# A post-norm decoder layer on one core: PSUM banks dealt by block, smaller stages in another order, layer norms applied on ScalarE

## What is computed

```
x = layernorm(x + attn(x))          # 8-bit rounded activations, sign weights; 16 heads of 32;
                                    # softmax over the HEADS of one token, plus a recurrent state:
                                    # out = softmax(q k^T) v + q @ kv_state   (a state per 128-token chunk)
                                    # then rmsnorm, 8-bit rounding and a sign-weight projection
x = layernorm(x + xattn(x, ctx))    # 32 query heads, 8 kv heads of 16, window 64, keys from ctx and x
x = layernorm(x + ffn(x))           # x @ base_w^T + bias + 2.0 * LoRA, top 2 of 8 experts by softmax gate
```

## Time and profile before

| | us |
|---|---|
| median of 3 runs | 1296.49 (1296.21 to 1297.39) |
| the profiled execution, by its own clock | 1297.64 |
| its span, first to last instruction | 1295.5 |
| PE busy | 923.4 (71%) |
| DVE busy | 551.9 (43%) |
| ACT busy | 286.3 (22%) |
| POOL busy | 87.0 (7%) |
| mean granted clock of TensorE | 0.812 of full speed |

### The profile page before, as it was taken

One profiled execution on the slowest core, in us unless ns is written; L12 is line 12 of the kernel. 1 busy time (PEld: TensorE's weight loads), 2 busy tenths in 40 slices (PEclk: granted clock), 3 DMA queues, 4 the chain that ended last, 5 costly groups with the idle time before them and its releaser, 6 DMA issues.

```text
span 1295.5 us, 23211 instructions
## 1 busy us (share of the span) xinstructions
PE 923.4 (71%) x10038; PEld 604.3 (47%) x10038; DVE 551.9 (43%) x1105; ACT 286.3 (22%) x549; POOL 87.0 (7%) x103
## 2 busy tenths in 40 slices
PE   2555865867687777867777867778767876778575
PEld 2342753356434653356433754356533664355323
DVE  3425145442644346443644247443545336132322
ACT  4112212412042111412032211401132210411220
POOL 0101001010001001010001001010000100000001
PEclk9756886988888867988778877988779787888686
DMA  9501000000000000000000000000000000000000
GB/s 315 137 2 33 2 1 1 1 33 2 17 1 34 2 1 17 2 34 2 1 17 26 9 2 17 1 34 2 2 17 17 1 2 17 2 1 1 17 1 17
DMA packets 18818, 27.15 MB, mean 21 GB/s; under 512 B 5401, under 2 KB 7577, under 8 KB 18721
## 3 DMA queue, kind: packets, MB, share of 16 engines
q1 hardware_dynamic: 18432, 24.84, 6.1%
q10 hardware_dynamic: 288, 0.80, 0.2%
HBM read 21.44 MB, written 4.19 MB: 20 GB/s over the span
## 4 chain that ended last, share of the span: by engine, by line
PE 41%; issue 30%; DVE 18%; ACT 7%; POOL 2%; DMA 2%; DVEq 0%; POOLq 0%; SPq 0%; ACTq 0%
PE ps L859 9%; DVE max_b L1181 4%; PE ps L899 4%; PE ps L869 3%; ACT p_b L648 2%; PE ps L879 2%; PE ps L832 2%; PE ps L776 2%; PE ps L805 2%; PE ps L808 2%; PE ps L932 2%; PE ps L796 2%; PE ps L964 1%; ACT p_a L599 1%; DVE x L1157 1%
## 5 line engine op out<-in xcount | busy, mean ns | idle before, releaser
L1181 DVE TENSOR_REDUCE max_b<-ps 128x4 f32<-128x768 f32 (+2 forms) x160 | 105.7, 711 | 128.8 <-PE ps L913 67.7
L899 PE MATMUL ps<-k_b,q_b 32*128 32x192 f32 (+2 forms) x1024 | 77.3, 432 | 104.5 <-DVE max_b L1181 84.3
L648 ACT ACTIVATE p_b<-ps 128x512 f32<-128x512 f32 (+1 forms) x256 | 118.5, 549 | 123.7 <-PE ps L941 123.7
L899 PEld LDWEIGHTS ps<-k_b,q_b 32*128 32x128 f32 x1024 | 54.4, 249 | 129.2 <-DVE max_b L1181 95.5
L932 PE MATMUL ps<-q_b,k_b 32*128 32x512 f32 (+1 forms) x512 | 76.8, 674 | 32.9 <-ACT p_b L648 31.3
L1066 DVE SCALAR_TENSOR_TENSOR nat<-ps,st_a,qkv_bias 128x512 f32<-128x512 f32 x48 | 35.6, 746 | 115.8 <-PE ps L729 115.8
L964 PE MATMUL ps<-wo,o_fb 128*128 128x512 f32 x128 | 68.4, 695 | 20.5 <-DVE o_fb L1218 20.5
L859 PE MATMUL ps<-c_t,wq 128*128 128x256 f32 x256 | 70.8, 439 | 6.7 <-ACT wq L570 6.7
L1003 PE MATMUL ps<-base_t,x_t 128*128 128x512 f32 x128 | 73.5, 706 | 0.0
L957 PE MATMUL ps<-p_b,v_b 128*32 128x256 f32 (+1 forms) x1024 | 66.1, 379 | 2.4 <-ACT p_b L648 2.4
L859 PE MATMUL ps<-x_t,wq 128*128 128x256 f32 x256 | 66.2, 416 | 0.0
(11 more groups left out here) (174 smaller groups left out, 1545.1 us busy)
## 6 DMA issues: line engine op xcount, KB each, us to landing
x_in<-x SPq DMA_DIRECT2D x8, 512.0 KB, 3.7
c_in<-ctx SPq DMA_DIRECT2D x8, 512.0 KB, 4.4
y<-x SPq DMA_DIRECT2D x8, 512.0 KB, 2.8
p_b<-L_attn_qkv_w SPq DMA_DIRECT2D x3, 1024.0 KB, 7.2
p_b<-L_xattn_Wq SPq DMA_DIRECT2D x1, 2048.0 KB, 10.8
p_b<-L_attn_proj_w SPq DMA_DIRECT2D x1, 1024.0 KB, 9.7
p_b<-L_ffn_base_w SPq DMA_DIRECT2D x1, 1024.0 KB, 8.9
wo<-L_xattn_Wo SPq DMA_DIRECT2D x8, 128.0 KB, 8.9
```

The lines of the kernel that those rows point to most:

```text
L648: act.activation(p_b[:, j % 2, s, 0:cols], bank(4 + s)[:, 0:cols], ACT.Exp, scale=DB ** -0.5).then_inc(pb_here.sem, 1)
L899: pe.matmul(bank(4 + r)[:, (i % 2) * N:(i % 2) * N + 2 * n * S], q_b[strip[r], i, :, :].rearrange("p h q -> p (h q)"), k_b[strip[r], half, ...
L1181: ins = dve.tensor_reduce(max_b[:, half, 0, i:i + k, 2 * n:2 * n + 2], ps[:, 4 + 2 * n:6 + 2 * n, :].rearrange("p r (i n) -> p i r n", i=2 ...
```

## The change

- **Banks.** Everything of the first attention's chain (`a1` transposes, all six `a1_qkv` products, the state, `a3_t`, both halves of `a3`) goes through bank 0. Everything of the feed-forward part (`c1_x2`, `c1`, gates, both halves of `c2`) goes through bank 1. Each of these products now waits for the reader of the one before. The second attention keeps 4 to 7.
- **Order.** All engines' lists are rewritten. The second attention's `b4` and its norm move from lag B into the next step, lag C; the norm of the first attention moves from A into the next step, lag B. Stages are split so that other work can stand between their parts (`b1_q` by pairs of k, `b1_k` by source, `b2` on DVE by reduction, `b3` on DVE in three, `c1` on DVE in two, `a2_rec` and `a3_ms` by themselves).
- **Norms.** DVE no longer applies them. It makes shift = -mean * rstd (a 128 x 2 operation) and ACT does `Identity` with a scale and a bias per row, for x1, x2 and y.
- **Other moves.** The two roundings go from DVE to POOL, as two 128 x 512 operations each instead of one of 128 x 1024; the copies of the state and of `v_b` go from DVE to ACT. On SP the load of ctx is issued ahead of the load of x.

```
@@ pool @@
+                x_scaled(pool, b)
+                oq_turn.before(pool, b)
+                for t in range(T):
+                    ins = pool.tensor_scalar(xq[:, t, :], y_a[:, t, :], MAGIC, MAGIC, ALU.add, ALU.subtract)
+                ins.then_inc(x_round.sem, 1)
...
@@ scalar @@
+            def norm_apply(z, rs, row, dst, t):
+                return act.activation(dst[:, t, :], z[:, t, :], ACT.Identity, scale=rs[:, row + 1, t:t + 1], bias=rs[:, row + 2, t:t + 1])
+            def b4_x2(b, t):
+                    sh_here(act, b)
+                    y_sent.before(act, b)
+                    norm_apply(x1, rs_b, 0, x2, t).then_inc(x2_here.sem, 1)
+            def c2_y(b):
+                sc_here(act, b)
+                for t in range(T):
+                    ins = norm_apply(z_c, rs_c, 0, z_c, t)
+                ins.then_inc(y_here.sem, 1)
...
-            run(act, [(C_, c1_x2), (B, b1_x1), (C_, c1), (A, a1_q), (A, a1_v),
+            run(act, [(A, a1_state), (A, a1_q), (B, of(b1_c, 0)), (B, of(b1_c, 1)), (A, a1_v), (A, of(a2_m, 0)), (C_, of(b4_x2, 0)),
...
@@ tensor @@
-                    if n >= 2:
-                        nat_here(pe, b, n - 1)
+                    else:
+                        nat_here(pe, b, n)
...
-                        mm = pe.matmul(bank(1 - n % 2), xq_t[:, k, t * P:(t + 1) * P], qkv_sign[:, k, w * C:(w + 1) * C],
+                        mm = pe.matmul(bank(0), xq_t[:, k, t * P:(t + 1) * P], qkv_sign[:, k, w * C:(w + 1) * C],
...
+            def a1_qt(b):
                 nat_here(pe, b)
+                if not (isinstance(b, int) and b < 3):
+                    zc_here(pe, b - 3)
...
-                    mm = pe.matmul(bank(t), xq_t[:, k, t * P:(t + 1) * P], proj_sign[:, k, :], start=(k == 0), stop=(k == KT - 1))
+                    mm = pe.matmul(bank(0), xq_t[:, k, t * P:(t + 1) * P], proj_sign[:, k, :], start=(k == 0), stop=(k == KT - 1))
...
+            def c1_x2(b, t):
                     x2_here(pe, b, t + 1)
+                    if t:
+                        x2t_here(pe, b, 1)
...
-                        mm = pe.transpose(bank(6 + t)[:, k * P:(k + 1) * P], x2[:, t, k * P:(k + 1) * P], eye)
+                        mm = pe.transpose(bank(1)[:, k * P:(k + 1) * P], x2[:, t, k * P:(k + 1) * P], eye)
...
             def c2(b, t, half):
-                if t and half == 0:
-                    gmt_here(pe, b)
+                if half == 0:
+                    if t == 0:
+                        gmt_here(pe, b)
+                    else:
+                        zc_here(pe, b, 1)
...
-            run(pe, [(C_, c1_x2), (B, of(b1_q, 0, range(KT))), (B, b1_x1), (C_, c1), (B, of(b1_q, 1, range(KT))),
+            run(pe, [(B, b1_c), (A, a1_state), (A, a1_qt), (C_, of(b4, 1, 0)), (C_, of(b4, 0, 0)), (C_, of(b4, 0, 1)), (A, of(a1_v, 0)),
...
@@ vector @@
+            def norm_shift(b, mv, rs, row, rstd, done):
                 rstd(dve, b)
+                dve.scalar_tensor_tensor(rs[:, row + 2, :], mv[:, :, 0], -1.0, rs[:, row + 1, :], ALU.mult, ALU.mult).then_inc(done.sem, 1)
...
-            run(dve, [(C_, c1), (A, a1_state), (A, of(a1_t8, 1, (2,))), (A, of(a2_max, 0)), (B, b1_v), (A, of(a2_out, 0)), (A, of(a2_max, 1)),
+            run(dve, [(C_, of(b4_z, 1)), (C_, b4), (A, of(a2_max, 0)), (C_, b4_x2), (A, of(a2_out, 0)), (NEXT, a0), (A, of(a2_max, 1)),
```

More of the change, by code:

```diff
@@ L712, in a1 @@
                 x_round(pe, b)
[L713 to L714 removed]
+                za_here.before(pe, b)
                 for t in range(T):
```

257 lines of the change are left out of this document (129 added, 128 removed).

## The result

The changed kernel takes **1050.41 us** (median of 4 runs, 1047.31 to 1064.07) against 1296.35 us for the kernel before beside it: ratio 0.8105, 95% interval 0.8077 to 0.8132. Forecast were 1125 us and a range of 1070 to 1195. So the direction was right and the size was not: 246 us saved, 171.5 forecast.

What follows compares the result with a forecast made beforehand. PE and its hand-overs to readers bound the kernel, not DMA. Savings of 12 (start, step 1), 123 (steps 2 to 6), 26 (step 7), 15 (step 8), less 4.5 (step 9), sum to 171.5: 1125 us, range 1070 to 1195.

Steps and rivals of the forecast that it cites:

- the allowance for the low clock: Time added for PE at half clock: 3.5 us in the rest stretch; pairs of `b2` at 3.76 us, against 3.25 at full clock.
- the rest stretch: All of a step outside the maxima pairs and the `b3` rounds: from 71.9 us to 55, most PE waits covered.
- The first and the third rival: Clock stays poor, low share 36%: step 131 us, 1181, chance 0.17; hand-overs keep clock low: step 162, 1397, chance 0.08.
- `b2`, 39 forecast: Maxima pairs, from 45.6 us to 39: six pairs 22.6, two short 5.6, two transpositions 6.5, the rest gates and hand-overs.
- The gate operations: In `b2`, 17 operations on DVE between the halves, with PE waiting behind them: 2 to 3 us.
- The bank 0 hand-over and the product longer than its gap: In `b2`, one exposed hand-over of bank 0 and one product that outlasts its gap: 2 us more.
- `b3`, 29 forecast: The eight `b3` rounds, from 31.5 us to 29: rounds stay at 3.71 us, the bf16 transposes stand in front.
- One bank for a chain: Five `a1_qkv` hand-overs of 1.1 us each, covered by other products and counted at nothing; without cover 5.5 us a step.
- Norms on ScalarE: ACT's Identity for x1, x2 and y at 0.63 us each, 3.8 us a step on an engine mostly idle.
- Rounding on POOL: Two chunks at 695 ns each, covered in the loop even at twice that; 1 us in the start.
- The end: Step 8 saves 15 us; step 9, now with the last projection and one bank each, costs 4.5 us.
- the three signs of being wrong: Clock at or below 0.82, PE waiting over 3 us a step on bank 0's readers, or seam q transposes waiting for DVE.

Runs made afterwards that it cites:

- e6_fill_before: The kernel before, with 12 products a step whose results nobody reads, put in TensorE's waits: 1258.30 us, ratio 0.9718.
- e13_seam_fill5: e5_seam with unread products in its seam, 4 ahead of the output projection and 5 behind it: 1168.73 us, ratio 0.9043.
- e5_seam: The changed kernel with the seam between two steps (x2 transposes, output projection) put back as in the kernel before: 1210.99 us, ratio 0.9339.
- e4_two_banks_start: The changed kernel with the start's qkv products alternating between banks 0 and 1, the loop unchanged: 1035.31 us, ratio 0.8006.
- e3_norm_dve: The changed kernel with its layer norms applied on VectorE again, at the same places of the order: 1048.40 us, ratio 0.8102.
- e2_round_dve: The changed kernel with both roundings back on VectorE, one 128x1024 operation each: 1048.01 us, ratio 0.8095.

## Why the prediction was wrong, by its own steps

By stretch, at profile spans (1295.5 against 1050.4): steps 2 to 6 saved 189.4 us where 123 were forecast, step 7 35.2 against 26, the start with step 1 17.9 against 12, steps 8 and 9 together 2.6 against 10.5. So the miss lies in the step: 109.7 us where I said 123. The direction and the mechanism, waits at the seam and in the first attention that other work covers, were right; terms of the sum were not. In the step of 110.3 us shown above, the rest came out 4.9 us shorter than forecast, `b2` 6.1 and `b3` 1.7. Two steps of the prediction failed: the allowance for the low clock, and the terms of `b2` for work and hand-overs that turned out to be covered.

- **The low clock.** For the rest stretch I had 47.5 us of products, 4 of exposed waits and 3.5 for a lower clock; measured are 46.8 busy, 3.3 idle and a clock of 1.00, so 50.1 us and not 55. Over the whole step I said clock 0.86 to 0.89 and PE busy about 105, for which the prediction has no working; measured are 0.95 and 97.0. So 8 of the 13 us by which a step was missed are busy time, 5 are idle time. The first and the third rival, which let the clock stay or fall, were wrong in the same place, and further. My error was to take the clock of the present step as a property of its kind of work. What that clock is worth show e6_fill_before and e13_seam_fill5, 6.1 us a step each.
- **Where the clock still falls.** In the step from 685.1 to 795.4 it falls once, at 744 us, behind the first of the two longest waits below (1.90 us) and ahead of the second, and it is back by 758. In each of the five steps it falls once, 0.4 to 2.2 us behind the end of this wait; waits of up to 1.2 us in the rest and in `b3` do not bring it down. The Trainium skill (TensorE: Matmul & The Clock Gate, "A second HAM failure mode: psum-queue depth-cycling") describes a kernel whose clock swings between its levels because of short idle times between groups that cycle through PSUM banks; the traces here don't show that of the hand-overs of banks 0 and 1, only the fall in `b2`.

```profile
743.64 1.30 PE L940 MATMUL ps<-k_b,q_b 32*128 32x192 f32 x16 [1.90 <-DVE max_b L1201]
...
748.49 1.03 PE L961 MATMUL ps<-cb,maxq_b 128*128 128x128 bf16 x8 [2.05 <-DVE maxq_b L1216]
...
753.90 1.66 PE L940 MATMUL ps<-k_b,q_b 32*128 32x192 f32 x16 [0.61 <-DVE max_b L1201]
...
757.99 0.93 PE L940 MATMUL ps<-k_b,q_b 32*128 32x192 f32 x16
```

- **`b2`, 39 forecast, 32.9 measured.** Six pairs 23.4 (22.6 forecast, so here the allowance for the low clock was not too large), two short ones 4.85 (5.6), two transpositions of the maxima 4.6 (6.5, the second is wholly covered by feed-forward and qkv products). The gate operations, for which I had 2 to 3 us, cost nothing: they end on DVE at 752.4 us and DVE then waits 0.3 us for PE. The bank 0 hand-over and the product longer than its gap, 2 us together, cost 0.4. And the waits for maxima are not "about as long in sum as now", but 3.6 us a step against 10.1, as the transposes of x2, the router product and the projection run in them. New is a wait of 2.6 us a step for the transposed maxima of the first half, which feed-forward products used to cover.
- **`b3`, 29 forecast, 27.3 measured**; rounds of 3.7 us, as forecast (771.84 to 775.55), at clock 1.00.
- **Seam.** The mechanism stands: the waits for `o_fb` and the norm are gone. What I had not seen is how much hangs on it. Its saving in my sum is the 17 us of the rest stretch; e5_seam shows 23.2: 17.9 in the rest, 3.4 in `b2`, which lacks the transposes of x2 as filler there and has clock 0.76 in place of 0.79, and 1.5 in `b3`, where one more half of the feed-forward product stands there, at clock 1.00 in both.
- **One bank for a chain**, counted at nothing in the loop beside the one hand-over in `b2`: right, 0.4 us a step. In the start I gave it no price of its own; there it costs 17 us (e4_two_banks_start). Step 1 was to start at about 124 us; its ctx transposes start at 141.0, where the kernel before has 120.4, and step 1 itself is what saves time.
- **Norms on ScalarE.** Taken at 0.63 us each, they took 0.80 to 0.83; the Trainium skill's 799 ns (ScalarE: Activation LUTs, "What ACT_TABLE_LOAD costs") agrees with the trace. The dearer norms made nothing slower, as e3_norm_dve shows.
- **Rounding on POOL.** Taken at 695 ns a chunk, it took 1.93 us. The bound of twice that, 1.39, was short too, and the start loses 6.5 us by it up to step 1 (e2_round_dve; 4 by the medians), not 1: TensorE waits 12.5 us for the rounded output there, against 8.7 before. In the loop it is covered, as said.
- **The end.** Step 9's extra serial work was forecast at 4.5 us and step 8's saving at 15; together they saved 2.6 and not 10.5. But a step now begins ahead of the 7.3 us of projection that used to end the one before it (5.32 and 1.98 us in the step shown). Without this shift the two save about 10, and the start with step 1 about 11 in place of 17.9, near the 10.5 and 12 forecast. For the start that is luck: one bank cost 17 us and the rounding 6.5 that the sum didn't have, and step 1 saved that much more (130.8 us to 108.0 from one start of the ctx transposes to the next).
- **Numbers of the prediction that don't follow.** The rivals start from a step of 113 us without low clock. The sum's own allowances are 3.5 us in the rest and 3.1 for six pairs (3.76 - 3.25 each), which leaves 116.4; the first rival would then be at 135 a step. The lower end of my own range, 1075, was put down to 5 us a step, which over seven steps gives 1090. And none of the three signs of being wrong came: the clock was above 0.82, the waits for bank 0's readers under 3 us, and the transposes of q at the seam didn't wait for DVE. They looked only for a slower kernel, and the miss was on the other side.

The forms that the points on ScalarE and POOL rest on: norms on ACT, rounding and scaling on POOL.

```profile
L635 ACT ACTIVATE x<-out_a,rs_a 128x512 f32<-128x512 f32 x16 | 12.3, 828 | 0.1
...
L635 ACT ACTIVATE x<-x,rs_b 128x512 f32<-128x512 f32 x16 | 12.1, 803 | 10.7 <-DVE rs_b L1185 10.7
```

```profile
L528 POOL TENSOR_SCALAR xq<-nat 128x512 bf16<-128x512 f32 x16 | 30.6, 1927 | 2.5 <-POOL nat L522 2.5
...
L522 POOL TENSOR_SCALAR nat<-out_a,st_a 128x512 f32<-128x512 f32 x16 | 10.9, 693 | 26.8 <-DVE st_a L1164 26.8
```
